# A recurrent layer with two steps in flight, and the experts' stores moved to SyncE's queue

## The reference

```python
x = x + _L0_ffn_ref(_layernorm(x), router_w, expert_bias, w_gate, w_down, ...)   # 160 experts, 8 a token
x = x + _L0_attn_b_ref(_layernorm(x), Wg, Wc, w1, w2, w3, ln_w, ffn_w)
x = x + _L0_ffn_ref(_layernorm(x), ...)                                          # the same weights

def _L0_attn_b_ref(inp, Wg, Wc, w1, w2, w3, ln_w, ffn_w):
    norm_inp = rmsnorm(inp, ln_w)
    beta = sigmoid(norm_inp @ Wg.T)
    hx_hat = norm_inp @ Wc.T
    h[t] = (1 - beta[t]) * h[t - 1] + beta[t] * hx_hat[t]        # a scan over the tokens
    h_norm = rmsnorm(h, ffn_w)
    return h + (silu(h_norm @ w1.T) * (h_norm @ w3.T)) @ w2.T
```

## Time and profile before

| | us |
|---|---|
| median of 3 runs (3164.58 to 3166.65) | 3166.4 |
| the profiled execution | 3175.44 |
| its span, first to last instruction | 3173.6 |
| PE busy | 1657.7 (52%) |
| DVE busy | 1390.8 (44%) |
| ACT busy | 958.2 (30%) |
| POOL busy | 1066.0 (34%) |

### The profile page before, as it was taken

How to read it: one execution, slowest core, us unless ns; L and a number is a source line. 1 busy time by engine, 2 the same in 40 slices (tenths; PEclk the granted TensorE clock), 3 DMA queues, 4 the chain that set the end, 5 groups by cost and what they waited for, 6 DMA issues and landing times.

```text
span 3173.6 us, 40197 instructions
## 1 busy us (share of the span) xinstructions
PE 1657.7 (52%) x13844; PEld 1113.4 (35%) x13844; DVE 1390.8 (44%) x3634; ACT 958.2 (30%) x1731; POOL 1066.0 (34%) x1177
## 2 busy tenths in 40 slices
PE   4763113229466633423333294656322456988985
PEld 2552112117344411311222173444211443454454
DVE  3548223213133444744442131334443466676655
ACT  3640000015222312111200042223258833344344
POOL 1003753640344265266336503452562020000001
PEclk9975555559777855555555597778665776898998
DMA  8991111339577611011013296767110000000000
GB/s 243 273 346 35 52 38 50 121 114 380 197 236 221 230 44 38 19 62 41 22 49 118 100 360 210 243 219 247 42 44 20 1 0 1 1 1 1 1 2 28
DMA packets 276792, 352.95 MB, mean 111 GB/s; under 512 B 68624, under 2 KB 161104, under 8 KB 276432
## 3 DMA queue, kind: packets, MB, share of 16 engines
q10 hardware_dynamic: 83984, 153.13, 13.8%
q1 hardware_dynamic: 159840, 130.08, 13.5%
q0 software_dynamic: 32768, 67.17, 6.8%
HBM read 201.35 MB, written 167.51 MB: 116 GB/s over the span
## 4 chain that ended last, share of the span: by engine, by line
PE 31%; issue 18%; DVE 17%; another core or an unknown queue 17%; ACT 12%; DMA 3%; SPq 1%; POOL 1%; ACTq 0%; DVEq 0%; POOLq 0%
ACT arena L1043 5%; PE psum L2159 5%; PE psum L2149 4%; PE psum L2110 4%; PE psum L448 3%; DMA arena<-expert_blocks 2%; PE psum L1494 2%; PE psum L1475 2%; PE psum L432 1%; PE psum L427 1%; ACT arena L1345 1%; PE psum L1491 1%; DVE X L1909 1%; PE psum L1492 1%
## 5 line engine op out<-in xcount | busy, mean ns | idle before, releaser
L1939 POOL DMA_INDIRECT arena<-slot_results,SLOTS x512 | 489.1, 955 | 729.0 <-DMA slot_results<-arena 326.5
L1928 POOL DMA_INDIRECT slot_rows<-arena,SLOTS x512 | 502.4, 981 | 522.2 <-issue 437.2
L1893 DVE COPY arena<-psum 128x512 f32<-128x512 f32 x288 | 195.7, 689 | 827.9 <-remote 521.3
L2149 PE MATMUL psum<-arena 128*64 128x128 f32 x2304 | 224.7, 324 | 299.4 <-issue 288.8
L1982 ACT ACTIVATE arena<-psum 128x512 f32<-128x512 f32 x288 | 172.0, 597 | 679.1 <-remote 304.6
L2159 PE MATMUL psum<-arena 64*128 64x128 f32 x2304 | 239.8, 335 | 206.6 <-issue 130.3
L2159 PEld LDWEIGHTS psum<-arena 64*128 64x128 f32 x2304 | 178.9, 218 | 269.4 <-issue 200.2
L2149 PEld LDWEIGHTS psum<-arena 128*64 128x64 f32 x2304 | 144.9, 158 | 362.8 <-issue 347.3
L2110 PE MATMUL psum<-ident,arena 128*128 128x128 f32 x1152 | 223.1, 325 | 15.7 <-DMA arena<-slot_rows 14.0
L169 POOL TENSOR_SCALAR rstd<-mv 128x4 f32<-128x4 f32 x32 | 6.8, 212 | 637.7 <-DVE mv L581 637.4
L1909 DVE SCALAR_TENSOR_TENSOR X<-arena,WEIGHTS,X 128x128 f32<-128x128 f32 x512 | 179.6, 352 | 27.9 <-DVE X L1909 5.9
(11 more groups left out here) (252 smaller groups left out, 3120.8 us busy)
## 6 DMA issues: line engine op xcount, KB each, us to landing
arena<-slot_rows ACTq DMA_DIRECT2D x288, 256.0 KB
slot_results<-arena ACTq DMA_DIRECT2D x288, 256.0 KB
arena<-expert_blocks SPq DMA_DIRECT2D x512, 96.0 KB
slot_rows<-zeros SPq DMA_DIRECT2D x2, 18432.0 KB, 79.9
arena<-own_blocks SPq DMA_DIRECT2D x44, 256.0 KB
slot_rows<-arena,SLOTS POOLq DMA_INDIRECT x512
arena<-slot_results,SLOTS POOLq DMA_INDIRECT x512
expert_blocks<-in_expert_w SPq DMA_DIRECT2D x1, 7680.0 KB, 26.1
```

Of the source, the lines that this page charges most:

```text
L1893: dve.tensor_copy(YSB[:, p].rearrange("p (c h) d -> p h c d", h=2), psum[:, first:first + 2, 0:256].rearrange("p h (c d) -> p h c d", c=2) ...
L1928: pool.indirect_dma_start(out=slot_rows[h], out_offset=bass.IndirectOffsetOnAxis(ap=slots_of(t, k), axis=0), in_=XNH[:, t], in_offset=None ...
L1939: pool.indirect_dma_start(out=GATHERED[:, n % TPI, k], out_offset=None, in_=slot_results[h], in_offset=bass.IndirectOffsetOnAxis(ap=slots_ ...
L2149: mm = pe.matmul(psum[lo:lo + INTER, 2 + 5 * (p % 2), o:o + P], gate_of(g, q), XSBT[:, p % 2, P * q:P * q + P], start=True, stop=True, ski ...
```

## The change

In the recurrent layer the engines' orders are written for a run of steps (0 to 3, then 4 to 7) rather than for one step, so that step i + 1 is projected and scanned, and step i + 2 scaled and transposed, while step i's gates and results are computed. `HX` has two buffers. `1 / rms` is applied per token: the products up have tokens in the partitions (`HX` as stationary operand, `w1` and `w3`, scaled by `ffn_w` once, as moving one), the mean square comes from four products with one column, root and reciprocal are of four columns, and ScalarE's Silu and VectorE's product take it as a scale. Four transposes (`turn`) and a copy (`turned`) bring the gates back. `beta` is computed by Tanh, and 1 - beta by Abs of it. Six of the summed tiles stay in steps 0 to 3 where ten were; seven are in the routing of the first half where four were; one more stands ahead of step 4. In the experts, the store of a group is issued by SyncE, behind the weights that wait for the same group, and not by ScalarE.

```diff
@@ -610,109 +610,210 @@
...
-        def glru_vector(dve, i, run, ahead, between):
...
-        def glru_scalar(act, i):
...
-        def glru_tensor(pe, i, between):
...
+        def glru_weights(dve):
+            dve.tensor_scalar(wc_t[:], wc_t[:], 0.5, None, ALU.mult)
+            dve.tensor_scalar(w13[:].rearrange("p a b -> p (a b)"), w13[:].rearrange("p a b -> p (a b)"), ffn_w[:, 0:1], None, ALU.mult)
+        def glru_vector(dve, first, last, run, between):
+            def stats_of(i):
+                summed(dve, TPI * i + TPI - 1, run)
+                front_stats(dve, i, GLRU)
+            def scale(i):
+                invert(dve, i, GLRU)
+                front_scale(dve, i, GLRU)
+            def scan(i):
+                dve.wait_ge(g_beta.sem, g_beta.at(0, i))
+                dve.scalar_tensor_tensor(BETA, BETA, 1.0, psum[:, 2, :], ALU.add, ALU.mult).then_inc(g_hx.sem, 1)
+                dve.wait_ge(g_hx.sem, g_hx.at(0, i, 1))
+                dve.wait_ge(g_y.sem, g_y.before(0, i - 1))
+                stand(dve)
+                for b in range(2):
+                    s = slice(SEQ * b, SEQ * b + SEQ)
+                    dve.tensor_tensor_scan(HX[:, i % 2, s], KEEP[:, s], BETA[:, s], 0.0, ALU.mult, ALU.add).then_inc(g_hx.sem, 1)
+            def root(i):
+                dve.wait_ge(g_rms.sem, g_rms.at(0, i, 1))
+                dve.reciprocal(RMS[:], RMS[:]).then_inc(g_rms.sem, 1)
+            def gates(i):
+                dve.wait_ge(g_up.sem, g_up.at(0, i))
+                dve.wait_ge(g_rms.sem, g_rms.at(0, i))
+                for j in range(TPI):
+                    dve.wait_ge(g_sil.sem, g_sil.at(0, i, j + 1))
+                    up = psum[:, 4, tile_of(j)]
+                    dve.scalar_tensor_tensor(GATE[:, tile_of(j)], up, RMS[:, j:j + 1], GATE[:, tile_of(j)], ALU.mult, ALU.mult).then_inc(g_gate.sem, 1)
+            def add(i):
+                dve.wait_ge(g_y.sem, g_y.at(0, i))
+                xs = X[:, TPI * i:TPI * i + TPI, :].rearrange("p t d -> p (t d)")
+                dve.tensor_tensor(xs, psum[:, 6, :], xs, ALU.add).then_inc(g_link.sem, 1)
+            for i in range(first, first + 2):
+                stats_of(i)
+                scale(i)
+            scan(first)
+            for i in range(first, last):
+                if i + 2 < last:
+                    stats_of(i + 2)
+                root(i)
+                if i + 2 < last:
+                    scale(i + 2)
+                if i + 1 < last:
+                    scan(i + 1)
+                between(i, 0)
+                gates(i)
+                between(i, 1)
+                add(i)
+                between(i, 2)
+            dve.wait_ge(g_link.sem, g_link.at(0, last - 1))
+        def glru_scalar(act, first, last):
+            def spread(i):
+                deviations(act, i, GLRU, both_eps[:, 0:1], RMS_EPS)
+            def tokens(i):
+                act.wait_ge(f_xt_ps.sem, f_xt_ps.at(GLRU, i))
+                act.wait_ge(g_proj.sem, g_proj.before(0, i))
+                act.activation(XT[:], psum[:, 0, :], ACT.Copy, scale=rms_w[:, 0:1]).then_inc(f_xt.sem, 1)
+            def beta(i):
+                act.wait_ge(g_proj.sem, g_proj.at(0, i))
+                act.wait_ge(g_hx.sem, g_hx.before(0, i))
+                act.activation(BETA, psum[:, 1, :], ACT.Tanh, scale=0.5).then_inc(g_beta.sem, 1)
+                act.wait_ge(g_beta.sem, g_beta.at(0, i, 1))
+                act.activation(KEEP, BETA, ACT.Abs, scale=0.5, bias=minus_half[:, 0:1]).then_inc(g_beta.sem, 1)
+            def squares(i):
+                act.wait_ge(g_hx.sem, g_hx.at(0, i))
+                act.wait_ge(g_ms.sem, g_ms.before(0, i))
+                act.activation(HSQ, HX[:, i % 2], ACT.Square).then_inc(g_sq.sem, 1)
+            def root(i):
+                act.wait_ge(g_ms.sem, g_ms.at(0, i))
+                act.wait_ge(g_gate.sem, g_gate.before(0, i))
+                act.activation(RMS[:], psum[:, 5, 0:TPI], ACT.Sqrt, bias=rms_eps[:, 0:1], scale=1.0 / D).then_inc(g_rms.sem, 1)
+            def gates(i):
+                act.wait_ge(g_up.sem, g_up.at(0, i))
+                act.wait_ge(g_rms.sem, g_rms.at(0, i))
+                act.wait_ge(g_tr.sem, g_tr.before(0, i))
+                for j in range(TPI):
+                    up = psum[:, 3, tile_of(j)]
+                    act.activation(GATE[:, tile_of(j)], up, ACT.Silu, scale=RMS[:, j:j + 1]).then_inc(g_sil.sem, 1)
+            def turned(i):
+                act.wait_ge(g_tr.sem, g_tr.at(0, i))
+                act.wait_ge(g_y.sem, g_y.before(0, i))
+                act.activation(GT, psum[:, 5, :], ACT.Copy).then_inc(g_gt.sem, 1)
+            spread(first)
+            tokens(first)
+            spread(first + 1)
+            beta(first)
+            for i in range(first, last):
+                if i + 1 < last:
+                    tokens(i + 1)
+                squares(i)
+                if i + 2 < last:
+                    spread(i + 2)
+                root(i)
+                if i + 1 < last:
+                    beta(i + 1)
+                gates(i)
+                turned(i)
+        def glru_tensor(pe, first, last, between):
+            def project(i):
+                pe.wait_ge(f_xt.sem, f_xt.at(GLRU, i))
+                pe.wait_ge(g_beta.sem, g_beta.before(0, i))
+                if i:
+                    pe.wait_ge(g_hx.sem, g_hx.at(0, i - 1, 1))
+                pe.matmul(psum[:, 1, :], wg_t[:], XT[:], start=True, stop=True)
+                pe.matmul(psum[:, 2, :], wc_t[:], XT[:], start=True, stop=True).then_inc(g_proj.sem, 1)
+            def up(i):
+                pe.wait_ge(g_gate.sem, g_gate.before(0, i))
+                for j in range(TPI):
+                    pe.wait_ge(g_hx.sem, g_hx.at(0, i, j // 2 + 2))
+                    for m in range(2):
+                        mm = pe.matmul(psum[:, 3 + m, tile_of(j)], HX[:, i % 2, tile_of(j)], w13[:, m], start=True, stop=True, skip_group_check=True)
+                mm.then_inc(g_up.sem, 1)
+            def squares(i):
+                pe.wait_ge(g_sq.sem, g_sq.at(0, i))
+                pe.wait_ge(g_gt.sem, g_gt.before(0, i))
+                for j in range(TPI):
+                    mm = pe.matmul(psum[:, 5, j:j + 1], HSQ[:, tile_of(j)], ones[:, 0:1], start=True, stop=True, skip_group_check=True)
+                mm.then_inc(g_ms.sem, 1)
+            def turn(i):
+                pe.wait_ge(g_gate.sem, g_gate.at(0, i))
+                for j in range(TPI):
+                    mm = pe.transpose(psum[:, 5, tile_of(j)], GATE[:, tile_of(j)], ident[:])
+                mm.then_inc(g_tr.sem, 1)
+            def results(i):
+                if i:
+                    pe.wait_ge(g_link.sem, g_link.at(0, i - 1))
+                pe.wait_ge(g_gt.sem, g_gt.at(0, i))
+                for j in range(TPI):
+                    pe.matmul(psum[:, 6, tile_of(j)], HX[:, i % 2, tile_of(j)], ident[:], start=True, stop=False, skip_group_check=True)
+                    mm = pe.matmul(psum[:, 6, tile_of(j)], GT[:, tile_of(j)], w2_t[:], start=False, stop=True, skip_group_check=True)
+                mm.then_inc(g_y.sem, 1)
+            front_tensor(pe, first, GLRU)
+            project(first)
+            front_tensor(pe, first + 1, GLRU)
+            for i in range(first, last):
+                up(i)
+                squares(i)
+                if i + 1 < last:
+                    project(i + 1)
+                between(i, 0)
+                if i + 2 < last:
+                    front_tensor(pe, i + 2, GLRU)
+                between(i, 1)
+                turn(i)
+                results(i)
+                between(i, 2)
...
@@ -1988,10 +2089,6 @@
                 act.wait_ge(c_y.sem, c_y.at(hr, 0, g - 1))
                 act.activation(HEB[:, g % 2], psum[:, 2 + 5 * (g % 2), 0:256], ACT.Silu).then_inc(c_he.sem, 1)
-            def store(g):
-                act.wait_ge(c_ysb.sem, c_ysb.at(hr, 0, g + 1))
-                act.dma_start(rows_of_group(slot_results[h], GROUP_ORDER[g]), YSB[:, g % UNROLL]).then_inc(c_st[g % UNROLL].sem, 16)
-
             for j in range(TPI):
                 act.wait_ge(d_rows[h][j].sem, d_rows[h][j].end(run))
             for g in range(UNROLL):
@@ -2004,9 +2101,6 @@
                     transposed(g + 2)
                 if g + 1 < GROUPS:
                     gated(g + 1)
-                if g:
-                    store(g - 1)
-            store(GROUPS - 1)
@@ -2025,9 +2119,12 @@
                 for q, e in zip(range(GROUP), experts):
                     sp.dma_start(EWB[:, p, q], expert_blocks[bass.ds(e * P, P), :]).then_inc(c_more[p].sem, 16)
-            sp.wait_ge(o_expert.sem, o_expert.at(run, h))
-            for m, g in enumerate(BROUGHT):
-                n, p = GROUP_ORDER[g], m % UNROLL
+            def store(g):
+                sp.wait_ge(c_ysb.sem, c_ysb.at(hr, 0, g + 1))
```

(58 more changed lines are left out.)

119 lines of the change are left out of this document (28 added, 91 removed).

## The result

Timed as the kernel before was, the changed kernel takes 3193.3 us (median of 4 runs, 3182.4 to 3195.8) against 3166.5 us: ratio 1.0071, 95% interval 1.0049 to 1.0093. I had forecast 3139 us. The executions profiled differ by less, spans of 3173.6 and 3180.5 us: the one of the kernel before is 9 us over its median, the one of the changed kernel 11 us under it. The later runs came from four chips, and these are of two kinds: on two of them the kernel before takes 3167 to 3189 us, as above, on the two others 2478 to 2481 us. On one of the latter two the changed kernel was run, and there it is 2% faster. What tells the two kinds apart decides this case.

A forecast was written before the change was run, and what follows sets the result against it. Full DMA engines and TensorE bound the full-speed experts, a serial chain and late signals the recurrent layer. Layer 39 - 10 + 6 = 35, less 8 for stores: 27 us off 3175.4, less 9.0, gives 3139 us; range 3092 to 3192.

The forecast's parts named there:

- old layer undisturbed, both halves: Recurrent layer: four old steps without lateness take 115 us in the first half, 112 in the second.
- new layer undisturbed: Recurrent layer: four new steps without lateness take 96 us in the first half, 92 in the second.
- gain of the layer, clock included: Recurrent steps: 39 us saved by the shorter loop, plus 6 us from a higher TensorE clock.
- moved sums: Routing before step 4: four summed tiles moved out of steps 0 to 3 cost 10 us.
- late signals: Recurrent steps: 130 us of lateness could fall by 22 us or grow by 26; taken as 0.
- stores: Experts: stores issued by SyncE behind weights cost 10 us, less 2 us credit beside gathers; net 8 us.
- Rival B: Recurrent layer: clock gives 30 us, lateness falls 22, stores cost only 2; 3087 us in all; chance 17%.
- my mark of 160: Recurrent steps: forecast wrong if late signals take over 160 us of the two stages.
- Rival C: Recurrent layer: each TensorE signal costs its own delay, 26 us more lateness; 3165 us in all; chance 11%.
- three signs of being wrong: Recurrent loop over 26 us, its late signals over 160 us, or VectorE waiting over 60 us for stores in 718 to 812.
- what I said would show the forecast: Loop 20 to 23 us, step stages 145 and 173, routing between near 106, full-speed expert groups 1.9 to 2.0 us.
- rival D: Experts: SyncE becomes the bound, late stores cost 73 us; 3204 us in all; chance 17%.

The follow-up runs named there:

- e13: Kernel before, unchanged, profiled on a chip without late signals: 2477.5 us.
- e16: Changed kernel as it is, on a chip without late signals: 2430.4 us, 0.9798 of the kernel before.
- e4: Changed recurrent layer, stores on ScalarE, GpSimd's second dispatch held back until the recurrent layer ended, on a chip with late signals: 3201.4 us.
- e11: Changed recurrent layer, stores on ScalarE, GpSimd stops after each tile's eight DMAs until landed, chip with late signals: 2822.2 us, 0.885 of the kernel before.
- e3: Kernel before, with GpSimd's second dispatch held back until the recurrent layer ended, on a chip with late signals: 3239.8 us.
- E0: Not a run but a stage: experts of the first mixture's first half; 260 us in the kernel before, 266 in the changed one, chip with late signals.
- e2: Kernel before, with only the stores moved to SyncE, on a chip with late signals: 3195.7 us, 1.0059 of the kernel before.
- e12: Changed kernel with SyncE issuing the store ahead of the weights, chip with late signals: 3200.7 us against the changed kernel's 3200.2.
- e14: Changed recurrent layer, stores on ScalarE, GpSimd waits only for the tile before, chip without late signals: 0.9786 of the kernel before.
- e9: Changed kernel run again on another chip with late signals: 3200.2 us, 1.0033 of the kernel before.
- e1: Changed kernel with the stores back on ScalarE, chip with late signals: 3169.2 us, 0.9983 of the kernel before.
- e17: Changed recurrent layer, stores on ScalarE, GpSimd waits only for the tile before, chip with late signals: 1.0031 of the kernel before.
- e10: Changed recurrent layer with stores on ScalarE, chip with late signals: 3172.9 us, 0.9970 of the kernel before.
- e18: Changed recurrent layer, stores on ScalarE, GpSimd stops after every second tile, chip with late signals: 2965.3 us, 0.937 of the kernel before.

## Why the prediction failed, step by step

Late = stage on the chip of the first timing less the same stage without late signals (e13, e16). That takes the chips to be alike in all else; e4 and e11 say so for the new layer (82 us in GB on late chips, 86 in e16), e3 for the old one (121, and 122 in e13).

| | forecast | measured |
|---|---|---|
| old layer undisturbed, both halves | 115 + 112 | 114.7 + 121.9 |
| new layer undisturbed | 96 + 92 | 83.1 + 86.3 |
| gain of the layer, clock included | 39 + 6 | 67 |
| moved sums | -10 | -12.5 |
| late signals | 0 | -46 |
| stores | -8 | -19 |
| sum | 27 faster | 10 slower |

**The layer: right in direction, too small.** The old step was read rightly in the first half. In the second, step 4 took 35.3 us in e13 from statistics to statistics, with its places and slots; I had read step 6 alone. The new loop was put at 22.5 us with a tile and is 18: I priced TensorE at its lower clock, 3.4 us for the products up and 3.8 for a projection. The rows of e16's chain have both levels: 3.75 us for the products up of step 0, 1.79 in step 3. The squares, which I bounded by 1.7 us, take 1.50 and 0.80. The granted clock of steps 0 to 3 rises from 0.55 to 0.65 undisturbed and from 0.57 to 0.63 where signals are late. Rival B had this right in direction: the clock gives more than 6 us, though no run parts its share of the 67 from the shorter loop's. In this program Tanh and Silu share no table: each has its load of 1.28 us in each of the eight steps.

**Moved sums: right.** 86.3 to 98.8 us in the routing.

**Late signals: the step that failed.** "Nothing decides between them, and I take 0." They rose from 161 to 207 us over the four stages: GA 49 to 50, RA 12 to 20, GB 69 to 84, RB 31 to 54. In the steps alone they are 133 us, 118 before (I had put 130), and my mark of 160 wasn't reached. What I left out are the routings: 42 to 73 us. The new steps 4 to 7 finish while the dispatch, 160 us of issuing, still runs (1348.9 to 1552 us, the routing from 1521), so its rest falls on the routing. Rival C, a price for each signal, comes nearest with 26 us, but its mechanism isn't what the runs show: e4 has the lateness go wherever GpSimd's stretch goes, and in the stretch from 1425.6 to 1590 us it holds back nearly all the work put beside it.

None of my three signs of being wrong came: the loop is 18 us and not over 26, the lateness in the two stages 133 us and not over 160, VectorE's wait for stores 52.1 us and not over 60. But of what I said would show the forecast, the routing (118.5 us for 106) and the pace of a group (2.08 us for 1.9 to 2.0) missed, and these are the two places of the loss.

**Stores: the second step that failed, by its size.** The lateness of stores was the mechanism I gave; its price lies between mine and rival D's. Forecast 0.1 us a group, net 8 us; measured 19. In the first profiles 0.16 and 0.11 us on 52 groups each, 14 us; the credit of 2 us beside the gathers isn't seen (E0 grows by 6.5 us in the profiles, by 10 in e2). That is far from D's 73 us. How much of a store's lateness TensorE's slack takes up wasn't measured by itself.
The Trainium skill (DMA: Bandwidth & Descriptors, queues, rings and completion order) has each DMA engine take turns between queue rows and consume one row's transfers in order. The traces are in keeping with that but don't prove it: weights and stores together take 66% of the engines' time on SyncE's queue, and with the store first (e12) the landing of weights stands in 23% of the chain. SyncE's own issuing would look alike.
On a chip without late signals the stores hardly count: e14, with them on ScalarE and the wait for the tile before, is 5 us faster than e16 beside it, and the two intervals overlap (0.9786 and 0.9798). The likely reason is that the experts run beside GpSimd's transfers for nearly their whole length there, some 64 of 72 groups, and have no backlog to work off at full speed; no run tests it.

**Sum.** 67 - 12.5 - 46 - 19 is 10 us of loss; e9 shows 11, e1 and e2 together 13. The 27 us of the first timing aren't explained in full; they rest on four executions of each kernel, and on one chip 13 executions of the kernel before lie between 3145 and 3184 us (beside e17). Its two profiles differ by 7 us, and not by these terms alone: the experts' four halves are only 3 us longer, and 15 us lie in the stretch behind them. That stretch takes 959 to 961 us in three traces with late signals (the kernel before, e10, e12) and 972 to 977 in the seven others without added stops in the gather (among them the changed kernel and e2, with the old layer), so it isn't the change that decides. Nearly all the difference arises 130 to 240 us into the stretch, where GpSimd's last gather ends. In the three short ones GpSimd stops by itself for 6 to 10 us some 170 us in, in the seven long ones for at most 4 us or not at all. That fits the hold on signals; no run was made to test it. Without late signals the stretch takes 905 us (e13, e16). The upper end of my range, 3192, missed the median by 1 us. That it came so near is luck: it stood for D, not for late signals in the routings.

## What to carry to other kernels

Idle time put down to "remote" or "issue" while GpSimd issues indirect DMAs one behind the other is a bound of its own. Find out first whether it goes away when GpSimd stops for a moment, before the work beside it is shortened: what is saved there is else paid out as waiting. On a chip of that kind a stop of 2 us for each eight DMAs gave 11.5%, the best version there; on one without late signals it cost 12%, and the changed kernel as it is (0.980) or the new layer with stores on ScalarE and the wait for the tile before (0.979) are the best. No version run here is best on both.

A DMA moved to another queue should be charged with what that queue's other traffic waits for, in both orders; and TensorE's work in a loop that gets tighter should be priced at both clock levels.

## What the runs showed of the hardware

**Chips differ by 22% on one kernel.** 2480 us against 3167 to 3189 us, with the same durations of instructions: an indirect DMA occupies GpSimd for a median of 0.95 us on either, ScalarE's 512-column copy takes 0.60. The difference is in TensorE's signals: up to 62 us late while GpSimd issues indirect DMAs without a stop, in the first timing and on two chips of the later runs; at most 0.1 us on two others. VectorE's are late too, by up to 9 us. Whether this belongs to the chip or to a state that it was in isn't shown: only one chip was met twice, and its signals were late both times.

**The hold is lifted when GpSimd stands still until its DMAs have landed.** With a stop of some 2 us after every 8 DMAs the latest signal is 7.9 us late (e11), with one after every 16 it is 21 us, 17 in the recurrent stages (e18); a wait that is already met does nothing (e17). In the held stretches TensorE's instructions themselves come 2.1 us apart. What resource is held, no run here shows. GpSimd's own stop of 24.7 us in the changed kernel, which awaits VectorE, lets the signals through as well, but the DMAs have time to land in it. So whether a short stop that doesn't await the landing, or other instructions of GpSimd between the DMAs, would do, is open; it wasn't tried.
